# Attention with routed experts on one core: experts computed for the tokens that chose them, in 15 sorted tiles

## The chip, the core and the metric

The kernel runs on one core of one Trainium2 chip. Times are device microseconds of one execution. Three runs of the kernel before gave 1228.81, 1231.50 and 1231.53 us, so its median is 1231.5 us. The profile is of one further execution.

## The reference

The input is 8 batches of 512 tokens with 128 features. Each batch goes through differential causal attention with 16 heads of 8 features, then a layer norm, then a mixture of 8 experts of which each token takes the best two, then a last layer norm. Everything is float32.

```python
attn = softmax(s1) - lam * softmax(s2)              # causal, 16 heads
attn = attn / max(sum(abs(attn)), 1e-6)
x = layernorm(x + (attn @ v) @ Wo.T)
xn = layernorm(x) * gamma + beta
probs = softmax(xn @ router_w.T / 1.5)
w, idx = top_k(probs, 2)                            # 2 of E = 8 experts
h = silu(einsum('btd,edf->betf', xn, W1))           # 128 -> 512, every expert
y = einsum('betf,efd->betd', h, W2)                 # 512 -> 128
x = layernorm(x + x + sum over e of wdense[e] * y[e])
```

## The kernel before, in words

One batch of attention is cut into 64 units, one for a head and a tile of 128 queries. The program of each engine is a list of passages, and a passage has 64 slots; slot s issues the scores of unit s on TensorE, and behind it, at fixed lags, the maximum (VectorE, line 723), the exponentials (ScalarE, line 491), the scaling and subtraction of the two maps (GpSimd, lines 441 and 445, five slots later, so slot s treats unit s-5), the transposes and the product with the values. A unit's width runs over 256, 128, 384 and 512 keys, four units of each in turn.

The rest of the work is side tasks, which a table SIDE puts into slots. A passage b holds the attention of batch b, the preparation of batch b+1 ("prep", slots 24 to 43) and everything behind the attention of batch b-1 ("post", slots 8 on). Post tasks whose slot is 64 or more run in the next passage ("late"), so the experts of a batch lie across two passages. TensorE and ScalarE do a side task in its own slot, VectorE one slot later and GpSimd two slots later (LAG_SIDE). Each engine's queue is in order: an instruction that waits holds back all that stands behind it on that engine. The first attention passage (batch 0) has no post work; after the eighth, a passage with the end of the attention pipeline and one with late tasks alone follow.

The experts before take each of the 8 experts over all 512 tokens: 32 tasks "hidden" (a 512-column matmul on TensorE, line 803; tanh on ScalarE, line 537; the product hT on VectorE, line 686) and 32 tasks "expert" (4 matmuls of 128 columns each, line 809; acc on VectorE, line 698, with the gate, which is zero for tokens that did not choose the expert). They fill about one per slot from slot 20 to slot 84. A float32 matmul shows as two matmul records in the trace. The experts' matrices are loaded once, 4 MB, and stay in SBUF.

SyncE issues all transfers. It writes the split projections to DRAM (line 390, 13 transfers a batch) and reads them back as stacks (line 398, 36 transfers a batch); each group of nine stack transfers waits until the scores that read its buffer are done.

## Time and profile before

| | |
|---|---|
| median of 3 runs | 1231.5 us |
| the profiled execution | 1223.18 us, span of the trace 1221.3 us, granted clock 0.952 |
| first maximum of batch 0 | 38.5 us |
| passages of batches 0 to 7 | 103.5, 135.2, 140.4, 140.3, 140.2, 142.5, 140.4, 134 us |
| after the last maximum | 106.3 us |

The profiled execution is 1.9 us longer than its span. The passages are cut at VectorE's first maximum of a batch. Engines are PE (TensorE matmul), PEld (its weight load), DVE (VectorE), ACT (ScalarE), POOL (GpSimd) and SPq (SyncE's queue).

### The profile page before, as it was taken

How to read it: one execution, taken by the hardware profiler on the slowest of the kernel's cores; microseconds unless marked ns; L12 is line 12 of the kernel's file. 1: busy time of each engine (PE TensorE's matmuls, PEld its weight loads, DVE VectorE, ACT ScalarE, POOL GpSimd, SP SyncE). 2: the span in 40 equal slices, each digit the busy share in tenths (PEclk: the TensorE clock that was granted, in tenths of full speed). 3: DMA queues.
4: the chain of work that ended last, by engine and by line, in shares of the span. 5: the costliest groups of instructions: out<-in, count | busy, mean ns of one | idle time of the engine just before them, and what ended most of it. 6: DMA issues, size and time to landing. Idle time of an engine off the chain costs nothing.

```text
span 1221.3 us, 29361 instructions
## 1 busy us (share of the span) xinstructions
PE 1103.2 (90%) x8786; PEld 725.7 (59%) x8786; DVE 1044.4 (86%) x2722; ACT 915.2 (75%) x2882; POOL 834.0 (68%) x1245
## 2 busy tenths in 40 slices
PE   3788869999899989999899997999899998999897
PEld 1355536666556655666556665666556665566565
DVE  1688788988999899999999899999999999898664
ACT  1688868888688877888688876888678886787232
POOL 2599976776768757877667776777677777677100
PEclk8577779999999999999999999999999999999899
DMA  7503400232005200142003300052002410000000
GB/s 213 126 14 80 99 1 3 62 82 48 1 14 118 70 2 2 36 110 57 1 14 86 89 15 1 21 125 57 1 2 57 89 48 1 19 1 2 1 10 9
DMA packets 62142, 54.66 MB, mean 45 GB/s; under 512 B 6050, under 2 KB 59938, under 8 KB 61986
## 3 DMA queue, kind: packets, MB, share of 16 engines
q1 hardware_dynamic: 61986, 52.78, 17.8%
q8 instruction: 73, 1.20, 0.4%
q14 instruction: 83, 0.68, 0.2%
HBM read 37.03 MB, written 15.73 MB: 43 GB/s over the span
## 4 chain that ended last, share of the span: by engine, by line
PE 66%; DVE 18%; issue 7%; POOL 4%; ACT 2%; SPq 1%; DMA 1%; DVEq 0%; POOLq 0%; ACTq 0%
PE side L809 14%; PE side L803 13%; PE trans L883 12%; PE scores L853 8%; PE heads L872 7%; DVE neg_max L723 6%; PE scores L855 4%; DVE abs_sum L734 3%; PE scores L803 2%; PE scores L809 2%; POOL exps L445 2%; PE side L773 2%; DVE hT L686 1%; DVE xh L566 1%; POOL exps L441 1%
## 5 line engine op out<-in xcount | busy, mean ns | idle before, releaser
L491 ACT ACTIVATE exps<-scores,neg_max 128x256 f32<-128x256 f32 (+3 forms) x1024 | 537.9, 529 | 97.5 <-DVE neg_max L723 80.8
L723 DVE TENSOR_REDUCE neg_max<-scores 128x1 f32<-128x256 f32 (+3 forms) x1024 | 448.7, 479 | 72.8 <-PE scores L855 69.3
L445 POOL TENSOR_TENSOR exps<-exps 128x384 f32<-128x384 f32 (+3 forms) x512 | 444.7, 868 | 42.7
L441 POOL TENSOR_SCALAR exps<-exps,inv_l,lam_l 128x384 f32<-128x384 f32 (+3 forms) x512 | 313.6, 613 | 141.2 <-DVE inv_l L714 138.4
L853 PE MATMUL scores<-stack 72*128 72x256 bf16 (+3 forms) x1024 | 274.1, 314 | 17.5 <-DMA stack<-parts_dram 13.5
L809 PE MATMUL side<-w_sb,hT 128*128 128x128 f32 x1816 | 253.6, 283 | 29.5 <-DVE acc L698 18.1
L883 PE MATMUL trans<-ident,exps 128*128 128x128 f32 x1280 | 254.9, 300 | 22.8 <-ACT diffT L499 19.4
L499 ACT ACTIVATE diffT<-trans 128x384 f32<-128x384 f32 (+3 forms) x512 | 223.4, 436 | 52.9 <-PE trans L883 52.1
L809 PEld LDWEIGHTS side<-w_sb,hT 128*128 128x128 f32 x1816 | 222.6, 192 | 63.7 <-DVE acc L698 29.9
L803 PE MATMUL side<-xnT,w_sb 128*128 128x512 f32 x458 | 247.2, 621 | 1.8 <-ACT xnT L526 1.0
L883 PEld LDWEIGHTS trans<-ident,exps 128*128 128x128 f32 x1280 | 150.4, 147 | 134.7 <-issue 102.5
L855 PE MATMUL scores<-causal_bf,ident_bf 128*128 128x128 bf16 x1024 | 216.5, 228 | 0.0
L491 ACT ACTIVATION_READ_ACCUMULATOR exps<-scores,neg_max 128x1 f32 x1024 | 210.7, 206 | 0.0
L734 DVE TENSOR_REDUCE abs_sum<-exps 128x2 f32<-128x512 f32 (+3 forms) x256 | 206.9, 808 | 1.7 <-POOL exps L445 1.7
L686 DVE SCALAR_TENSOR_TENSOR hT<-tanh_sb,side 128x512 f32<-128x512 f32 x229 | 155.8, 680 | 36.3 <-ACT tanh_sb L537 34.5
L537 ACT ACTIVATE tanh_sb<-side 128x512 f32<-128x512 f32 x229 | 136.1, 594 | 48.0 <-PE side L803 44.8
L853 PEld LDWEIGHTS scores<-stack 72*128 72x128 bf16 x1024 | 108.2, 106 | 64.1 <-ACT exps L491 22.8
L872 PE MATMUL heads<-diffT,v_sb 128*32 128x128 f32 x2560 | 139.2, 291 | 0.0
L872 PEld LDWEIGHTS heads<-diffT,v_sb 128*32 128x32 f32 x2560 | 51.0, 109 | 122.2 <-ACT diffT L499 61.4
L855 PEld LDWEIGHTS scores<-causal_bf,ident_bf 128*128 128x128 bf16 x1024 | 105.4, 103 | 7.7
L437 POOL TENSOR_TENSOR lam_l<-sums,lam_all 128x4 f32<-128x4 f32 x128 | 25.9, 203 | 91.1 <-ACT exps L491 90.7
L803 PEld LDWEIGHTS side<-xnT,w_sb 128*128 128x128 f32 x458 | 69.3, 191 | 15.0 <-DVE hT L686 2.7
(94 smaller groups left out, 685.2 us busy)
## 6 DMA issues: line engine op xcount, KB each, us to landing
stack<-parts_dram SPq DMA_DIRECT2D x288, 96.0 KB
parts_dram<-parts SPq DMA_DIRECT2D x104, 128.0 KB, 2.4
x_in<-x_dram SPq DMA_DIRECT2D x8, 256.0 KB, 4.5
w_sb<-w_dram SPq DMA_DIRECT2D x1, 2048.0 KB, 9.1
x_res<-x_dram SPq DMA_DIRECT2D x8, 256.0 KB, 4.5
o_dram<-y_out SPq DMA_DIRECT2D x8, 256.0 KB, 3.4
wq_sb<-wqT_dram SPq DMA_DIRECT2D x1, 64.0 KB
wq_sb<-wk1T_dram SPq DMA_DIRECT2D x1, 64.0 KB
```

What stands on the lines that cost most here:

```text
L441: nc.gpsimd.tensor_scalar(diff[:, q % 2, j, 0:w], exps[:, q % 2, 1, j, 0:w], inv_l2[:, q % 2, j:j + 1], lam_l1[:, q % 2, j:j + 1], ALU.mul ...
L445: nc.gpsimd.tensor_tensor(diff[:, q % 2, j, 0:w], diff[:, q % 2, j, 0:w], exps[:, q % 2, 0, j, 0:w], ALU.subtract).then_inc(diff_done.sem, 1)
L491: nc.scalar.activation(exps[:, q % 2, k, j, 0:w], scores[:, u % 2, k, 0:w], ACT.Exp, bias=neg_max[:, q % 2, j, k:k + 1], accum_out=sums[:, ...
L499: nc.scalar.activation(diffT[:, q % 2, j, 0:w], trans[:, 0:w], ACT.Copy)\
L723: nc.vector.tensor_reduce(neg_max[:, q % 2, j, k:k + 1], scores[:, u % 2, k, 0:w], AX.X, ALU.max, negate=True).then_inc(max_done.sem, 1)
L734: nc.vector.tensor_reduce(abs_sum[:, q % 2, j - 1:j + 1], diff[:, q % 2, j - 1:j + 1, 0:w], AX.X, ALU.add, apply_absolute_value=True).then ...
L803: last = nc.tensor.matmul(bank[:, :], w1_sb[:, e, f * P:(f + 1) * P], xnT[:, :], start=True, stop=True)
L809: last = nc.tensor.matmul(bank[:, 0:D], hT[:, e % 2, f, t * P:(t + 1) * P], w2_sb[:, e, f, :], start=(f == 0), stop=(f == NF - 1))
L853: nc.tensor.matmul(scores[:, u % 2, k, 0:w], stack[:, 0, QUAD * g + j, t * P:(t + 1) * P], stack[:, 1 + k, QUAD * g + j, 0:w], start=True, ...
L855: nc.tensor.matmul(scores[:, u % 2, k, w - P:w], ident_bf[:, :], causal_bf[:, :], start=False, stop=True).then_inc(score_done.sem, 1)
L872: last = nc.tensor.matmul(heads[k * STRIP:(k + 1) * STRIP, t * P:(t + 1) * P], v_sb[:, i, NG * k + g, :], diffT[:, q % 2, k, i * P:(i + 1) ...
L883: last = nc.tensor.transpose(trans[:, i * P:(i + 1) * P], diff[:, q % 2, j, i * P:(i + 1) * P], ident[:, :])
```

## The change

The experts now work on sorted tokens. After routing, "count" and "place" compute with small matmuls and seven vector operations where each of the 1024 (token, expert) pairs of a batch goes, and which expert owns each of 15 tiles of 128 rows. GpSimd scatters the normalised tokens with 8 indirect transfers of 128 rows into a DRAM tensor; SyncE reads it back in 4 transfers ("sorted"); TensorE transposes it in 4 tasks "turn". Each tile then has one "hidden" (4 matmuls of 128 columns), one "expert" (4 matmuls) and, on SyncE, one "weights": a register is read from SBUF and 512 KB of the owner's matrices are fetched into one of 3 buffers. The outputs are written to DRAM in 4 transfers ("y_out"), gathered by 8 indirect transfers and added with the gates in 8 "combine". 32 tasks hidden and 32 expert a batch become 15 and 15. SyncE's list is now also written by slots.

```diff
-FIRST_EXPERT_SLOT = 20
-EXPERT_TASKS = (1, 2, 1, 1, 1, 1, 1, 1, 0, 1, 1, 1, 1, 1, 1, 1)
+COUNT_SLOT, PLACE_SLOT, SCATTER_SLOT, FIRST_TILE_SLOT = 27, 29, 31, 42
+WEIGHTS_AHEAD = 3
...
+    put(COUNT_SLOT, "post", "count")
+    put(PLACE_SLOT, "post", "place")
+    for i in range(TOP * NT):
+        put(SCATTER_SLOT + i, "post", "scatter", i)
+    put(SCATTER_SLOT + TOP * NT + 1, "post", "sorted")
+    for j in range(WEIGHTS_AHEAD):
+        put(FIRST_TILE_SLOT - 6 + j, "post", "weights", j)
+    for c, chunk in enumerate(CHUNKS):
+        put(FIRST_TILE_SLOT - 1 + 2 * chunk[0], "post", "turn", c)
+    slot = FIRST_TILE_SLOT
+    for j in range(TILES + 1):
+        if j < TILES:
+            put(slot + 2 * j, "post", "hidden", j)
+        if j:
+            put(slot + 2 * j + 1, "post", "expert", j - 1)
+            if j - 1 + WEIGHTS_AHEAD < TILES:
+                put(slot + 2 * j + 2, "post", "weights", j - 1 + WEIGHTS_AHEAD)
+    for c, chunk in enumerate(CHUNKS):
+        put(slot + 2 * chunk[-1] + 5, "post", "y_out", c)
+    slot += 2 * TILES + 4
+    for i in range(TOP * NT):
+        put(slot + i, "post", "gather", i)
+        put(slot + i + 2, "post", "combine", i)
+    slot += TOP * NT + 2
+    put(slot, "post", "norm3")
...
+                if name == "sorted":
+                    sp.wait_ge(scattered.sem, scattered.after(n, TOP * NT))
+                    sp.wait_ge(turned.sem, turned.after(n - 1, len(CHUNKS)))
+                    for c in CHUNKS:
+                        sp.dma_start(xg[:, c[0]:c[-1] + 1, :], pools(x_sorted[c[0] * P:(c[-1] + 1) * P, :]))\
+                          .then_inc(sorted_in.sem, 16)
+                if name == "weights":
+                    j = task[2]
+                    if j == 0:
+                        sp.wait_ge(placed.sem, placed.after(n, 6))
+                    m, k = (n, j - WEIGHTS_AHEAD) if j >= WEIGHTS_AHEAD else (n - 1, TILES + j - WEIGHTS_AHEAD)
+                    sp.wait_ge(y_copied.sem, y_copied.after(m, k + 1))
+                    which = sp.value_load(owner_int[0:1, j:j + 1], min_val=0, max_val=E - 1)
+                    sp.dma_start(w12_sb[:, j % WEIGHTS_AHEAD, :],
+                                 w12[bass.ds(which, 1), :, :].rearrange("o p f -> p (o f)"))\
+                      .then_inc(weights_loaded[j % WEIGHTS_AHEAD].sem, 16)
+                if name == "y_out":
+                    c = CHUNKS[task[2]]
+                    for i in range(TOP * NT) if n else ():
+                        sp.wait_ge(gathered[i].sem, gathered[i].after(n - 1, 1))
+                    sp.wait_ge(y_copied.sem, y_copied.after(n, c[-1] + 1))
+                    sp.dma_start(pools(y_dram[c[0] * P:(c[-1] + 1) * P, :]), y_sorted[:, c[0]:c[-1] + 1, :])\
+                      .then_inc(y_sorted_out.sem, 16)
...
+                    for task, n, _ in side_tasks(b, stages, slot):
+                        if task[0] == "post":
+                            sorted_part(task[1], n, task)
+                        if task[1] == "proj":
+                            parts_part(n, task[2])
+                    if "prep" in stages and slot >= PREP_SLOTS[3] + 5 and slot - PREP_SLOTS[3] - 5 < NG - 1:
+                        stack_part(b + 1, slot - PREP_SLOTS[3] - 5)
+                    if "prep" in stages and slot == UNITS - 1:
+                        stack_part(b + 1, NG - 1)
...
+            sp.wait_ge(consts_made, CONSTS)
+            sp.dma_start(pools(x_sorted), xg[:, :, :]).then_inc(sorted_cleared, 16)
...
+                        if name == "scatter":
+                            i = task[2]
+                            if i == 0:
+                                pool.wait_ge(sorted_cleared, 16)
+                                pool.wait_ge(sorted_in.sem, sorted_in.after(n - 1, len(CHUNKS)))
+                                pool.wait_ge(placed.sem, placed.after(n, 5))
+                                pool.wait_ge(xh_done.sem, xh_done.after(n, 1))
+                            nc.gpsimd.indirect_dma_start(
+                                x_sorted[:, :], bass.IndirectOffsetOnAxis(ap=place_int[:, i:i + 1], axis=0),
+                                xh[:, i % NT, :], None).then_inc(scattered.sem, 16)
+                        if name == "gather":
+                            i = task[2]
+                            if i == 0:
+                                pool.wait_ge(y_sorted_out.sem, y_sorted_out.after(n, len(CHUNKS)))
+                                pool.wait_ge(combined.sem, combined.after(n - 1, TOP * NT))
+                            nc.gpsimd.indirect_dma_start(
+                                y_back[:, i, :], None, y_dram[:, :],
+                                bass.IndirectOffsetOnAxis(ap=place_int[:, i:i + 1], axis=0)).then_inc(gathered[i].sem, 16)
...
                         if name == "expert":
-
-                            e, t = task[2], task[3]
+                            j = task[2]
                             dve.wait_ge(psum_of(task).sem, psum_of(task).after(n, psum_count[task]))
-                            if e == 0:
-                                dve.wait_ge(route_step.sem, route_step.after(n, ROUTE_STEPS))
-                                dve.wait_ge(acc_set.sem, acc_set.after(n, 1))
-                            else:
-                                dve.wait_ge(expert_done.sem, expert_done.after(n, NT * (e - 1) + t + 1))
+                            dve.wait_ge(y_sorted_out.sem, y_sorted_out.after(n - 1, len(CHUNKS)))
+                            nc.vector.tensor_copy(y_sorted[:, j, :], bank[:, 0:D]).then_inc(y_copied.sem, 1)
+                        if name == "combine":
+                            i = task[2]
+                            t = i % NT
+                            dve.wait_ge(gathered[i].sem, gathered[i].after(n, 1))
+                            dve.wait_ge(route_step.sem, route_step.after(n, ROUTE_STEPS))
+                            dve.wait_ge(acc_set.sem, acc_set.after(n, 1))
+                            if i >= NT:
+                                dve.wait_ge(combined.sem, combined.after(n, t + 1))
                             nc.vector.scalar_tensor_tensor(
-                                out=acc[:, t, :], in0=bank[:, 0:D], scalar=gates[:, t, e:e + 1],
-                                in1=(acc if e else x1_twice)[:, t, :], op0=ALU.mult, op1=ALU.add).then_inc(expert_done.sem, 1)
+                                out=acc[:, t, :], in0=y_back[:, i, :], scalar=gates[:, i // NT, t:t + 1],
+                                in1=acc[:, t, :] if i >= NT else x1_twice[:, n % 2, t, :],
+                                op0=ALU.mult, op1=ALU.add).then_inc(combined.sem, 1)
...
+                if name == "turn":
+                    c = CHUNKS[task[2]]
+                    pe.wait_ge(sorted_in.sem, sorted_in.after(n, len(CHUNKS)))
+                    for i, j in enumerate(c):
+                        last = nc.tensor.transpose(bank[:, i * P:(i + 1) * P], xg[:, j, :], ident[:, :])
                 if name == "hidden":
-                    e, f = task[2], task[3]
-                    if isinstance(n, int) and n == 0 and e == f == 0:
-                        pe.wait_ge(experts_in, 2 * 16)
-                    pe.wait_ge(xnT_copied.sem, xnT_copied.after(n, 1))
-                    last = nc.tensor.matmul(bank[:, :], w1_sb[:, e, f * P:(f + 1) * P], xnT[:, :],
-                                            start=True, stop=True)
+                    j = task[2]
+                    w = j % WEIGHTS_AHEAD
+                    pe.wait_ge(turned.sem, turned.after(n, j // NT + 1))
+                    pe.wait_ge(weights_loaded[w].sem, weights_loaded[w].after(n, j // WEIGHTS_AHEAD + 1))
+                    for f in range(NF):
+                        last = nc.tensor.matmul(bank[:, f * P:(f + 1) * P], w12_sb[:, w, f * P:(f + 1) * P], xgT[:, j, :],
+                                                start=True, stop=True)
                 if name == "expert":
-                    e, t = task[2], task[3]
-                    pe.wait_ge(hidden_done.sem, hidden_done.after(n, NF * (e + 1)))
+                    j = task[2]
+                    pe.wait_ge(hidden_done.sem, hidden_done.after(n, j + 1))
                     for f in range(NF):
-                        last = nc.tensor.matmul(bank[:, 0:D], hT[:, e % 2, f, t * P:(t + 1) * P],
-                                                w2_sb[:, e, f, :], start=(f == 0), stop=(f == NF - 1))
+                        last = nc.tensor.matmul(bank[:, 0:D], hT[:, (n * TILES + j) % 2, f, :],
+                                                w12_sb[:, j % WEIGHTS_AHEAD, F + f * D:F + (f + 1) * D],
+                                                start=(f == 0), stop=(f == NF - 1))
```

The order of the instructions changes at these places.

GpSimd at slots 33 to 35, before: `exps` are the probability maps, four units of 512 keys.

```order
L437 TENSOR_TENSOR lam_l<-sums,lam_all 128x4
L441 TENSOR_SCALAR exps<-exps,inv_l,lam_l 128x512
L445 TENSOR_TENSOR exps<-exps 128x512
L441 TENSOR_SCALAR exps<-exps,inv_l,lam_l 128x512
L445 TENSOR_TENSOR exps<-exps 128x512
```

The same place of GpSimd after, where `xh` are the normalised tokens and `place_int` the row numbers:

```order
L533 TENSOR_TENSOR lam_l<-sums,lam_all 128x4
L537 TENSOR_SCALAR exps<-exps,inv_l,lam_l 128x512
L541 TENSOR_TENSOR exps<-exps 128x512
L557 DMA x_sorted_dram<-xh,place_int 1920x128
L537 TENSOR_SCALAR exps<-exps,inv_l,lam_l 128x512
L541 TENSOR_TENSOR exps<-exps 128x512
L557 DMA x_sorted_dram<-xh,place_int 1920x128
```

An indirect transfer now stands behind each of eight units, the last at slot 40, and the next unit stands behind it; eight gathers stand so at slots 14 to 21.

TensorE at slots 41 and 42, after, where `xg` are the sorted tokens, and the scores below the transposes are those of slot 42:

```order
L1031 MATMUL scores<-stack 128x384
L1033 MATMUL scores<-causal_bf,ident_bf 128x128
L973 MATMUL side<-ident,xg 128x128 x4
L1050 MATMUL heads<-diffT,v_sb 32x128 x4
L1061 MATMUL trans<-ident,exps 128x128 x2
L1031 MATMUL scores<-stack 128x384
L1033 MATMUL scores<-causal_bf,ident_bf 128x128
L1031 MATMUL scores<-stack 128x384
L1033 MATMUL scores<-causal_bf,ident_bf 128x128
L980 MATMUL side<-xgT,w_sb 128x128 x4
```

The transposes of the sorted tokens stand ahead of the scores of slot 42; before, one 512-column matmul of the experts stood there, which waited for nothing new.

SyncE at slots 46 to 50, after, with what each instruction waits for; `w_sb` is the tile's matrices:

```order
L434 TENSOR_LOAD owner_int [waits y_copied]
L434 ISA x2
L435 ISA
L435 DMA w_sb<-w_dram 128x1024
L462 DMA stack<-parts_dram 24x4x512 [waits score_done,parts_out]
L462 DMA stack<-parts_dram 24x4x512 x8
L434 TENSOR_LOAD owner_int [waits y_copied]
L434 ISA x2
L435 ISA
L435 DMA w_sb<-w_dram 128x1024
```

Before, SyncE had no experts' transfer behind the first load; now each tile's fetch waits for the output copy three tiles back, and stack transfers stand between two fetches.

## Rows read from the trace of the kernel before

**Rows 1.** the page's part 1: busy us, share of the span, instructions
```profile
PE 1103.2 (90%) x8786; PEld 725.7 (59%) x8786; DVE 1044.4 (86%) x2722; ACT 915.2 (75%) x2882; POOL 834.0 (68%) x1245
```

**Rows 2.** the page's part 4: the chain that ended last, by engine
```profile
PE 66%; DVE 18%; issue 7%; POOL 4%; ACT 2%; SPq 1%; DMA 1%; DVEq 0%; POOLq 0%; ACTq 0%
```

**Rows 3.** windows of two passages: length, busy PE to POOL, clock, DMA, GB/s
```profile
38.50:142.00 103.50, 92.45 (x667) 52.39 (x665) 87.10 (x209) 90.03 (x317) 89.39 (x136) 0.71 0.32 70
...
557.90:698.10 140.20, 132.30 (x1098) 88.08 (x1098) 129.64 (x341) 113.89 (x361) 103.83 (x154) 1.00 0.19 46
```

**Rows 4.** the second passage in four windows, slots 10 on first; columns the same
```profile
578.40:623.90 45.50, 38.85 (x323) 25.10 (x321) 42.69 (x136) 31.33 (x99) 29.88 (x46) 1.00 0.01 2
...
623.90:651.80 27.90, 27.51 (x219) 18.23 (x217) 26.37 (x64) 24.07 (x77) 22.68 (x29) 1.00 0.10 26
...
651.80:698.10 46.30, 45.69 (x385) 30.09 (x383) 42.51 (x100) 41.38 (x130) 34.60 (x55) 1.00 0.37 89
...
557.90:578.40 20.50, 20.25 (x178) 14.66 (x179) 18.07 (x47) 17.11 (x57) 16.68 (x26) 1.00 0.29 77
```

**Rows 5.** groups by shape: busy, mean ns, idle before, releasers
```profile
L809 PE MATMUL side<-w_sb,hT 128*128 128x128 f32 x1816 | 253.6, 283 | 29.5 <-DVE acc L698 18.1 <-DVE hT L686 5.5 <-issue 5.3
...
L803 PE MATMUL side<-xnT,w_sb 128*128 128x512 f32 x458 | 247.2, 621 | 1.8 <-ACT xnT L526 1.0 <-DVE hT L686 0.5
...
L445 POOL TENSOR_TENSOR exps<-exps 128x512 f32<-128x512 f32 x128 | 163.3, 1276 | 10.7
...
L464 POOL TENSOR_TENSOR rstd<-var_eps,minus_half 128x4 f32<-128x4 f32 x24 | 24.5, 1019 | 1.9
```

**Rows 6.** the same windows, the gated sum's first half alone (hT, line 686)
```profile
578.40:623.90 45.50, 5.41 (x8) 1.00 0.01 2
...
623.90:651.80 27.90, 4.77 (x7) 1.00 0.10 26
```

**Rows 7.** the same windows, accumulation over experts alone (acc, line 698)
```profile
578.40:623.90 45.50, 3.06 (x9) 1.00 0.01 2
...
623.90:651.80 27.90, 2.35 (x7) 1.00 0.10 26
```

**Rows 8.** line 398, issue of one stack transfer by SyncE: ns min/median/max
```profile
L398 SPq DMA_DIRECT2D stack<-parts_dram x288: 290/375/1662, 30.9 to 981.6; - x144
```

**Rows 9.** GpSimd's timeline, slots 33 to 40: first and last piece
```profile
636.08 0.77 POOL L441 TENSOR_SCALAR exps<-exps,inv_l,lam_l 128x512 f32<-128x512 f32 x1 [0.84 <-DVE inv_l L714]
...
651.12 0.73 POOL L445 TENSOR_TENSOR exps<-exps 128x256 f32<-128x256 f32 x1
```

**Rows 10.** the page's part 6: issues, KB of one, median us to landing
```profile
parts_dram<-parts SPq DMA_DIRECT2D x104, 128.0 KB, 2.4
...
x_in<-x_dram SPq DMA_DIRECT2D x8, 256.0 KB, 4.5
...
w_sb<-w_dram SPq DMA_DIRECT2D x1, 2048.0 KB, 9.1
...
o_dram<-y_out SPq DMA_DIRECT2D x8, 256.0 KB, 3.4
```

**Rows 11.** the chain in order of time, first transfer: start, us
```profile
7.88 2.79 DMA x_in<-x_dram
```

**Rows 12.** the timeline at slot 42: start, length, engine, operation
```profile
652.90 0.33 PE L853 MATMUL scores<-stack 72*128 72x384 bf16 x1
```

**Rows 13.** the timeline in slots 50 and 52: VectorE's side task, TensorE's
```profile
670.65 0.35 DVE L698 SCALAR_TENSOR_TENSOR acc<-side,gates,acc 128x128 f32<-128x128 f32 x1
...
674.57 1.07 PE L803 MATMUL side<-xnT,w_sb 128*128 128x512 f32 x2
```

**Rows 14.** windows of the end, after the last maximum; columns the same
```profile
1115.00:1151.00 36.00, 31.40 (x258) 22.13 (x256) 25.36 (x68) 14.77 (x33) 16.34 (x20) 1.00 0.00 1
...
1151.00:1215.00 64.00, 61.02 (x328) 42.99 (x328) 36.01 (x96) 19.38 (x34) 1.20 (x2) 0.95 0.02 5
```

**Rows 15.** line 566, normalising, the form that writes xh: ns min/median/max
```profile
L566 DVE TENSOR_SCALAR xh<-x,mv,rstd x32: 333/344/1432, 179.9 to 1149.2; 128x128 f32<-128x128 f32 x32
```

More of the change, by code:

```diff
@@ L104 @@
 PREP_TASKS = [t for s in sorted(SIDE) for t in SIDE[s] if t[0] == "prep"]
-PSUM_TASKS = ("den_T", "out_proj", "xn_T", "logits", "hidden", "expert", "x_T", "proj", "values")
+PSUM_TASKS = ("den_T", "out_proj", "xn_T", "logits", "count", "place", "turn", "hidden", "expert",
+              "x_T", "proj", "values")
+EXPERT_PSUM = ("turn", "hidden", "expert")
 STORED = (0, 1, 2, 0, 1)
@@ L284, in reader @@
                 "proj": (rest_made, task[2] + 1) if name == "proj" else None,
[L285 to L286 removed]
+                "count": (counted, 1), "place": (placed, 2),
+                "turn": (turned, task[2] + 1) if name == "turn" else None,
+                "hidden": (hidden_done, task[2] + 1) if name == "hidden" else None,
+                "expert": (y_copied, task[2] + 1) if name == "expert" else None,
             }[name]
@@ L309, in build @@
             for experts in (False, True):
-                chosen = [t for t in tasks if t[1] in PSUM_TASKS and (t[1] in ("hidden", "expert")) == experts]
+                chosen = [t for t in tasks if t[1] in PSUM_TASKS and (t[1] in EXPERT_PSUM) == experts]
                 for n, t in enumerate(chosen):
@@ L314, in psum_of @@
         def psum_of(task):
-            if task[1] in ("hidden", "expert"):
+            if task[1] in EXPERT_PSUM:
                 return expert_psum
@@ new lines, in side_task @@
+                if name == "place":
+                    pe.wait_ge(counted.sem, counted.after(n, 1))
+                    nc.tensor.matmul(bank[:, 0:NT * E], before[:, :], hit[:, 2, :, :], start=True, stop=False)
+                    for s in range(1, NT):
+                        nc.tensor.matmul(bank[:, s * E:NT * E], ones[:, :], hit[:, 2, 0:NT - s, :], start=False, stop=False)
+                    for k in range(NT):
+                        nc.tensor.matmul(bank[:, 0:NT * E], full[:, k, :], start_sb[:, 0:NT, :],
+                                         start=False, stop=(k == NT - 1))
+                    for k in range(NT):
+                        last = nc.tensor.matmul(bank[:, NT * E:(NT + 1) * E], full[:, k, :], start_sb[:, NT, :],
+                                                start=(k == 0), stop=(k == NT - 1))
```

235 lines of the change are left out of this document (153 added, 82 removed).

## The prediction

> **What bounds the kernel now.** I read the page's busy shares first: TensorE 90%, VectorE 86% of the span [rows 1]. The chain that ended last agrees: two thirds of it is TensorE [rows 2]. Then I cut one passage (batch 4, 140.2 us) into four windows [rows 3, 4]: slots 10 to 27, 28 to 40, 41 to 63, and 0 to 9. The reader should see three different limits. In slots 41 to 63 TensorE is busy 45.7 of 46.3 us, in 0 to 9 20.3 of 20.5: every microsecond that TensorE waits there is lost. In 10 to 27, where norms and routing lie, VectorE is busy 42.7 of 45.5. In 28 to 40 TensorE again has 27.5 of 27.9. The passage without experts (batch 0) takes 103.5 us, with GpSimd busy 89.4 of them [rows 3]: take the experts away and GpSimd is nearly the next limit, though it looks idle for a third of the time on the page.
>
> **What is removed.** 17 of 32 "hidden" and 17 of 32 "expert" a batch. One hidden costs TensorE two records of 0.54 us, one expert eight of 0.14 (busy by count) [rows 5], so about 1.1 us each: 37 us a batch. But the remaining 30 tasks keep one per slot, in slots 42 to 73. A tile's hidden is eight records of 128 columns, the shape of the expert row, thus 1.1 us as well. So in slots 41 to 63 and 0 to 9 TensorE has as much to do as before, and the saving lies only in slots 10 to 40.
>
> **Slots 10 to 27.** Without experts VectorE has 42.7 - 5.4 - 3.1 = 34.2 us [rows 4, 6, 7], plus 8 combines at 0.34, what each of nine cost before, = 36.9. GpSimd has 29.9 plus 8 gathers. What GpSimd pays for one indirect transfer of 128 rows no row shows. Lower bound 0.4 us, what SyncE spends on a stack transfer [rows 8]; upper bound 2.6 us, twice GpSimd's longest operation of 1.28 (a list for the source and one for the destination). I take 1.2, near its costliest operation on a tiny tile (1.02 for 128x4) and on a wide one (1.28) [rows 5]. So 29.9 + 9.6 = 39.5 us, and at the 92% busy that such a limit reaches, 43 instead of 45.5: **-2.5 us** a batch. Combines wait for gathers one slot after their issue; GpSimd is ahead often enough that I add nothing.
>
> **Slots 28 to 40 and the turn.** GpSimd did slots 33 to 40 from 636.1 to 651.9, the first four wide ones [rows 9]. Eight scatters add 9.6; 1.7 of gaps in it and 1.5 of an earlier start (28 to 32 have no experts) come off: the last scatter ends at 658.2. Its landing takes 2.4, as SyncE's writes to DRAM do; then four reads of 256 KB: issue 0.45 each, landing 2.8 alone to 4.5 behind others, 5.0 together [rows 10, 11]. At 665.6 the transposes of slot 41 may start, 0.6 us, and only behind them the scores of slot 42, which started at 652.9 [rows 12]. 666.2 - 652.9 = **+13.3 us**. All of attention is behind it: maxima, exponentials and, in its next group of four units, GpSimd. The time does not come back, since TensorE fills the slots after it. Even with scatters at no cost, landing and read-back alone leave some 5 us. Three more turns cost four transposes each, half an expert's records, 0.55: **+1.7**. Clearing and count and place hide under GpSimd's scatters.
>
> **The fetches.** A tile's matrices are asked for when the output three tiles back is copied, on VectorE in slot s, and needed by TensorE in slot s+2. Today the same places are 671.0 (end of a side task, slot 50) and 674.6 (slot 52): 3.6 us of cover [rows 13]. The fetch takes 0.1 for the semaphore, 0.6 for the register (no row; 0 to 2.4, a round trip to DRAM), 0.5 to issue, and 3.7 to land, between 2.8 for 256 KB and 9.1 for 2048 KB [rows 10, 11]: 4.9. The missing 1.3 us is paid on every second tile, since a wait at one gives cover to the next: 0.65 on 12 tiles (3 are fetched early) = 8. Twice a batch nine or eighteen stack transfers at 0.38 [rows 8] stand before a fetch on SyncE, 3.4 or 6.8 us, of which I count 5 in all. **+13 us**; 0 if all lands in 3.6, 23 if a landing takes 4.5 and the register 1.0.
>
> **The clock.** TensorE is granted 1.00 (2.4 GHz) where it is busy, and 0.71, a mixture with 1.2 GHz, in the passage without experts [rows 3]. Waits of ten microseconds and lighter slots invite that. I charge 6% on the 67 us of slots 41 to 63 and 0 to 9: **+4 us**, bounds 0 and 16 (granted 0.8).
>
> **Start and end.** Before the first load SyncE now waits for GpSimd's constants and clears 1 MB: +3. The end has no attention to hide in. It took 36 + 64 us [rows 14] and the last norm. The first 36 hold the previous batch's gathers: +5. In place of the 64 (routing, count and place are my estimates for some thirty short operations in a row): routing 7, count and place 5, scatters 9.6 + 2.4, read-back 5, turn 1.5, first tile 4. Then the loop: from one output copy over the fetch (4.9), the next hidden (1.1), the expert behind it (1.1) to a copy (0.3) passes 7.4 us and two tiles, 3.7 each, times 14 = 52. Writing back 3.9 with its issue (3.4 at landing [rows 10]), gathers 9.6 + 2.4. Together 103: +39, so **+44** in all.
>
> **Sum.** A full passage: -2.5 + 13.3 + 1.7 + 13 + 4 = 29.5, six times (batches 2 to 7) = 177. Batch 1's passage has no slots 0 to 9 with experts: 24. With 3 and 44: 248. 1221.3 + 248 + 1.9 outside the span = 1471 on the profiled execution's scale of 1223.2; the median of the runs is 0.7% above that: **1480 us**.
>
> **A rule against the change.** The norm that writes xh usually takes 0.34 us and up to 1.43 [rows 15]: beside a GpSimd operation it is held until that one ends. If every scatter and gather is held or holds by such a 1.1, it is 16 x 1.1 x 7 = 123 us more, 1600 instead of 1480; it belongs to rival 2. The Trainium skill (SBUF — State Buffer, section "Who interferes with whom") says that VectorE's copies and scalar operations on SBUF and GpSimd's work lock each other out for a whole instruction, the writing of descriptors too. By that rule, the trace agrees on the lock, and no run here shows descriptors.
>
> **Rivals.**
> 1. The fetches are hidden, because they land in 3.6 us. For it: 2.8 for 256 KB alone [rows 11]. Against: the stack transfers between. Then 13 x 6.7 = 87 falls away, and at the end 14 x (3.7 - 2.4) = 18, where 2.4 is TensorE's own work on a tile: 1375. Chance 0.15.
> 2. An indirect transfer holds GpSimd 2.5 us, by itself or held by VectorE. Scatters +10.4; slots 10 to 27 then need 29.9 + 20 = 50 on GpSimd, 52 long, +9: 19.4 x 7 and 16 x 1.3 at the end, 157 more: 1640. Chance 0.17.
> 3. The clock is granted 0.8 in the slots that TensorE fills: +12 x 6.7: 1560. For it is the 0.71 [rows 3], against it that these slots keep TensorE busy. Chance 0.10.
> 4. Not slower: the waits are absorbed, and the busiest engine sets the pace as TensorE does now (132 of 140). GpSimd would have 103.8 + 19.2 = 123, at 93% a passage of 132, -8 x 7, with the end +44 and start: 1222. It needs the wait at slot 41 to be covered, which decides at about zero between scatter and transposes. Against it: seven microseconds of landings between two tasks that now lie within one. Chance 0.07.
> The forecast itself, 1400 to 1560: 0.51.
>
> **Range and chances.** Single bounds: an indirect transfer at 0.4 takes off 8 x 0.8 and 3.7 (VectorE then bounds slots 10 to 27 at 39.3) seven times and 13 at the end, 1397; fetches hidden give 1375, both near 1300; 2.6 gives 1650; the dearer fetch 1560. 1340 to 1650 holds the forecast, rivals 1, 3 and most of 2. Faster by over 0.3% (about what a measurement can tell from no change) only by rival 4, which is near no change: 0.05, same 0.02, slower 0.93.
>
> **What would show it.** TensorE idle some 13 us at slot 41, ended by the read-back. Waits at hidden for the matrices, every second tile. GpSimd's indirect transfers near 1.2 us. Passages near 170 us, of which slots 10 to 27 give 43. The end from 106 to 150 us. The prediction is wrong if the passages stay near 140, above all if TensorE finds the sorted tokens there.

## The result, and the profile after

The changed kernel takes **1641.2 us** (median of 4 runs, 1638.7 to 1652.6) against 1230.4 before (1228.8 to 1231.5): ratio 1.336, 95% interval 1.329 to 1.343. That is 411 us slower; 249 were forecast. The size lies inside the range by 9 us, but two terms of the sum were wrong in kind, not only in size.

The page's part 1 and three lines of part 2 (tenths in 40 slices) for the changed kernel answer [rows 1]:

```profile
PE 1111.0 (68%) x8522; PEld 794.6 (49%) x8522; DVE 953.7 (58%) x2585; ACT 866.2 (53%) x2778; POOL 977.2 (60%) x1385
...
PE   2988766776578584784947849578476875788262
...
PEclk8678657976579755996568965689567985589577
DMA  4323015510354003540126401353014520133243
```

264 matmul records have gone, yet TensorE's busy time rose by 8 us: the granted clock fell from 0.95 to 0.74 as a mean over the span. No engine is above 68%. The chain that ended last, 66% TensorE before [rows 2], now names everybody:

```profile
PE 30%; POOL 21%; DMA 16%; DVE 12%; SPq 9%; issue 9%; ACT 1%; DVEq 0%; POOLq 0%; ACTq 0%
```

Batch 4's passage in the same four windows as [rows 4] (slots 0 to 9, 10 to 27, 28 to 40, 41 to 63; length, busy PE to POOL, clock, DMA share, GB/s):

```profile
712.40:739.60 27.20, 22.33 (x200) 18.63 (x198) 16.20 (x43) 16.87 (x56) 16.43 (x25) 0.87 0.41 116
739.60:795.90 56.30, 31.99 (x245) 19.78 (x243) 40.10 (x129) 28.45 (x97) 39.23 (x55) 0.66 0.07 19
795.90:831.10 35.20, 29.66 (x171) 19.34 (x171) 20.87 (x56) 20.42 (x68) 25.66 (x31) 0.60 0.12 36
831.10:913.30 82.20, 55.21 (x455) 42.75 (x453) 41.38 (x96) 42.25 (x131) 40.59 (x61) 0.80 0.54 141
```

The passage takes 200.9 us instead of 140.2 [rows 3]. All four parts are longer: by 6.7, 10.8, 7.3 and 35.9. The windows of [rows 4] do not begin quite at the slots: in the trace before, the first maximum of slot 10 is at 577.9 and that of slot 28 at 624.7, not at 578.4 and 623.9. Between equal slots the four parts are longer by 7.2, 9.5, 8.0 and 35.9; as means over batches 2 to 6 by 7.4, 9.2, 8.0 and 33.0. Where nothing else is said, the numbers below go by [rows 4], as the forecast did.

No engine is busy for more than 85% of any part, where before the busiest had 94 to 99%. So most of the extra time is waiting; in slots 28 to 40 TensorE is also slower, busy for 29.7 us with 171 records where it was busy for 27.5 us with 219. The view of waits (engine, tile, who was waited for: us in total, times, longest) says for what:

```profile
PE side L973 <- DMA xg<-x_sorted_dram: 103.5, 7, 15.4
DVE acc L852 <- DMA y_back<-y_sorted_dram,place_int: 101.8, 43, 5.0
...
PE side L980 <- DMA w_sb<-w_dram: 96.4, 37, 6.7
PE side L947 <- DVE xh L689: 75.2, 8, 12.3
...
DVE place_of L809 <- PE side L967: 27.0, 7, 3.9
...
PE scores L973 <- DMA xg<-x_sorted_dram: 20.7, 1, 20.7
```

Three waits of about 100 us each: the turn for the sorted tokens, the combines for their gathers, the tiles for their matrices. A fourth, TensorE's wait at slot 19 for the normalised tokens xh, was 18.1 us in 8 waits before; it follows from the second, as shown below. The 20.7 us are the turn of the last batch.

**The turn.** TensorE's timeline around slot 41 (start, us, engine, operation), then GpSimd's and SyncE's:

```profile
846.58 1.09 PE L973 MATMUL side<-ident,xg 128*128 128x128 f32 x4 [15.18 <-DMA xg<-x_sorted_dram]
...
848.66 0.53 PE L1031 MATMUL scores<-stack 72*128 72x384 bf16 x1
```
```profile
836.36 1.08 POOL L557 DMA_INDIRECT x_sorted_dram<-xh,place_int  x1 [0.16 <-issue]
```
```profile
840.35 2.04 SPq L426 DMA_DIRECT2D xg<-x_sorted_dram  x4
```

The last scatter's instruction ends at 837.4, the read is issued from 840.4, and the transposes start at 846.6: 9.1 us between. Slot 41 took 18.3 us instead of 1.9. Place stands in the same line, at 797.3, with 24 records of TensorE at half clock:

```profile
797.30 0.58 PE L960 MATMUL side<-hit,before 128*128 128x32 f32 x2
797.69 1.43 PE L962 MATMUL side<-hit,ones 128*128 128x24 f32 x6
799.05 1.91 PE L964 MATMUL side<-start_sb,full 8*128 8x32 f32 x8
800.77 1.85 PE L967 MATMUL side<-start_sb,full 8*128 8x8 f32 x8
```

They take 5.3 us, some 0.22 a record, though the widest moves 32 columns. In these 5.3 us the loading of TensorE's weights is busy for 5.25.

**The combines** on VectorE, slots 16 to 19:

```profile
765.29 0.62 DVE L852 SCALAR_TENSOR_TENSOR acc<-y_back,gates,x_twice 128x128 f32<-128x128 f32 x1 [4.52 <-DMA y_back<-y_sorted_dram,place_int]
...
769.95 0.75 DVE L852 SCALAR_TENSOR_TENSOR acc<-y_back,gates,acc 128x128 f32<-128x128 f32 x1 [2.52 <-DMA y_back<-y_sorted_dram,place_int]
```

and GpSimd at the same place:

```profile
760.31 0.78 POOL L537 TENSOR_SCALAR exps<-exps,inv_l,lam_l 128x512 f32<-128x512 f32 x1 [2.74 <-DVE inv_l L869]
761.17 1.27 POOL L541 TENSOR_TENSOR exps<-exps 128x512 f32<-128x512 f32 x1
762.59 1.04 POOL L565 DMA_INDIRECT y_back<-y_sorted_dram,place_int  x1 [0.15 <-issue]
```

Behind the waiting combines stand the maxima of the slots and the norm that writes xh, so ScalarE, GpSimd and TensorE wait as well. TensorE's part of it:

```profile
773.09 1.09 PE L947 MATMUL side<-ident,xh 128*128 128x128 f32 x4 [9.95 <-DVE xh L689]
```

A gather costs GpSimd as much as a scatter (ns min/median/max):

```profile
L557 POOL DMA_INDIRECT x_sorted_dram<-xh,place_int x64: 964/1082/1240, 221.2 to 1552.6; - x64
L565 POOL DMA_INDIRECT y_back<-y_sorted_dram,place_int x64: 945/1046/1257, 353.8 to 1627.8; - x64
```

**The fetches.** SyncE's queue in slots 50 to 54 and what TensorE waited for there:

```profile
868.04 6.61 SPq L462 DMA_DIRECT2D stack<-parts_dram  x15
875.69 3.52 SPq L435 DMA_DIRECT2D w_sb<-w_dram  x2
```
```profile
885.41 2.05 PE L980 MATMUL side<-xgT,w_sb 128*128 128x128 f32 x8 [6.48 <-DMA w_sb<-w_dram]
```
```profile
L434 SPq TENSOR_LOAD <-owner_int x120: 262/270/838, 216.8 to 1607.3; - x120
```
```profile
DMA to landing us min/median/max: 3.1/3.8/6.9
```

The last fence is the time from issue to landing, for the 40 of the 120 matrix loads whose landing the view gives; by the last landing mark of each, all 120 take 3.1 to 9.6 us, 3.7 in the middle. One fetch alone costs what was forecast: 0.3 for the register, 0.3 for the issue, 3.8 to land. The long wait comes where the stack transfers stand ahead of it, and there the fetch is late twice: the output it waits for was copied at 869.3, the fetch was issued at 875.7, behind them on SyncE, and it took 9.6 us to land, at 885.3, the longest of all.

### The profile page after: what moved, and what is told of

Read it like the earlier page. It is cut to its first block, busy times and chain, and to the rows that moved or that the text cites. A ratio compares the mean times of both kernels' runs of the same rounds, so it can differ in the third digit from the quotient of the medians.

```text
span 1637.5 us, 29253 instructions
## 1 busy us (share of the span) xinstructions
PE 1111.0 (68%) x8522; PEld 794.6 (49%) x8522; DVE 953.7 (58%) x2585; ACT 866.2 (53%) x2778; POOL 977.2 (60%) x1385
## 3 DMA queue, kind: packets, MB, share of 16 engines
q1 hardware_dynamic: 110866, 128.23, 27.8%
## 4 chain that ended last, share of the span: by engine, by line
PE 30%; POOL 21%; DMA 16%; DVE 12%; SPq 9%; issue 9%; ACT 1%; DVEq 0%; POOLq 0%; ACTq 0%
POOL exps L541 8%; DMA w_sb<-w_dram 8%; POOL exps L537 6%; PE side L980 5%; SPq L462 5%; PE trans L1061 5%; DVE neg_max L878 4%; PE scores L1031 4%; POOL x_sorted_dram L557 4%; PE heads L1050 3%; PE side L986 3%; DMA y_back<-y_sorted_dram,place_int 3%; DMA xg<-x_sorted_dram 2%; DMA x_sorted_dram<-xh,place_int 2%; PE scores L1033 2%
## 5 line engine op out<-in xcount | busy, mean ns | idle before, releaser
L1061 PE MATMUL trans<-ident,exps 128*128 128x128 f32 x1280 | 308.2, 351 | 141.5 <-ACT diffT L613 95.2
L1031 PE MATMUL scores<-stack 72*128 72x256 bf16 (+3 forms) x1024 | 327.2, 364 | 19.1 <-DMA stack<-parts_dram 15.8
L1033 PE MATMUL scores<-causal_bf,ident_bf 128*128 128x128 bf16 x1024 | 248.6, 257 | 0.0
L980 PE MATMUL side<-xgT,w_sb 128*128 128x128 f32 x864 | 140.8, 314 | 97.1 <-DMA w_sb<-w_dram 96.4
L980 PEld LDWEIGHTS side<-xgT,w_sb 128*128 128x128 f32 x864 | 123.0, 219 | 111.2 <-issue 106.4
L1031 PEld LDWEIGHTS scores<-stack 72*128 72x128 bf16 x1024 | 125.0, 122 | 78.8 <-ACT exps L605 32.8
L836 DVE SCALAR_TENSOR_TENSOR hT<-tanh_sb,side 128x512 f32<-128x512 f32 x108 | 74.2, 687 | 133.2 <-ACT tanh_sb L658 130.6
L658 ACT ACTIVATE tanh_sb<-side 128x512 f32<-128x512 f32 x108 | 64.5, 597 | 160.8 <-PE side L980 159.5
L986 PE MATMUL side<-w_sb,hT 128*128 128x128 f32 x864 | 131.1, 299 | 5.1 <-DVE hT L836 5.1
L1033 PEld LDWEIGHTS scores<-causal_bf,ident_bf 128*128 128x128 bf16 x1024 | 122.1, 119 | 15.7
L986 PEld LDWEIGHTS side<-w_sb,hT 128*128 128x128 f32 x864 | 116.1, 209 | 13.6 <-DVE hT L836 8.4
L565 POOL DMA_INDIRECT y_back<-y_sorted_dram,place_int x64 | 68.1, 1065 | 86.9 <-DMA y_sorted_dram<-y_sorted 75.5
```

What stands on the lines that cost most here:

```text
L980: last = nc.tensor.matmul(bank[:, f * P:(f + 1) * P], w12_sb[:, w, f * P:(f + 1) * P], xgT[:, j, :], start=True, stop=True)
L986: last = nc.tensor.matmul(bank[:, 0:D], hT[:, (n * TILES + j) % 2, f, :], w12_sb[:, j % WEIGHTS_AHEAD, F + f * D:F + (f + 1) * D], start=( ...
L1031: nc.tensor.matmul(scores[:, u % 2, k, 0:w], stack[:, 0, QUAD * g + j, t * P:(t + 1) * P], stack[:, 1 + k, QUAD * g + j, 0:w], start=True, ...
L1033: nc.tensor.matmul(scores[:, u % 2, k, w - P:w], ident_bf[:, :], causal_bf[:, :], start=False, stop=True).then_inc(score_done.sem, 1)
L1061: last = nc.tensor.transpose(trans[:, i * P:(i + 1) * P], diff[:, q % 2, j, i * P:(i + 1) * P], ident[:, :])
```

## The experiments

Each was timed beside the kernel before on the same chip, in three rounds (the last four in five); that kernel gave 1230.1, 1233.1 and 1234.5 us on the three chips used. Ratios to it have 95% intervals in brackets. "Less" is against 1641.2 us, or the run named, and across chips it is good to some 5 us.

**1. The combines three slots later** (and all that follows them):

```
- put(slot + i + 2, "post", "combine", i)      + put(slot + i + 5, "post", "combine", i)
- slot += TOP * NT + 2                         + slot += TOP * NT + 5
```

> Each combine stands three slots later behind its gather; nothing else moves. If the waits in line theory holds, VectorE's 102 us of waiting for gathers (43 waits, longest 5.0 us) were all on the path in slots 12 to 20: those slots fall from 33 us to about 24, and the time from 1641 to about 1570. If GpSimd's own work sets the pace there (16 indirect transfers of 1.07 us), the waits only move to another engine and the time changes by less than 15 us.

Measured: 1590.6 us, 1.292 [1.288, 1.296]: 51 less, 20 short of the 71 expected. The wait fell from 101.8 to 12.4:

```profile
DVE acc L852 <- DMA y_back<-y_sorted_dram,place_int: 12.4, 9, 4.9
```

Slots 16 to 19 went from 18.0 to 12.3 us, and TensorE's wait for xh from 75.2 to 40.0. The wait was real, but 89 us less of it were worth 51 us of time; some reappeared in other waits, the matrices' among them (96 to 103).

**2. The turn eight slots later**, and with it all that follows (tiles, gathers, combines), with gates and places in two buffers so that the next batch can write its own:

```
- FIRST_TILE_SLOT = 27, 29, 31, 42             + FIRST_TILE_SLOT = 27, 29, 31, 50
- gates = sb("gates", [P, TOP, NT])            + gates = sb("gates", [P, 2, TOP, NT])
- place_int = sb("place_int", [P, TOP * NT])   + place_int = sb("place_int", [P, 2, TOP * NT])
...
```

> The tiles and the first turn start 8 slots later (50 instead of 42), the scatters stay; gates and row numbers get two buffers. Waits in line theory: TensorE's wait for the sorted tokens, 15 us a passage (124 us in all), goes away in the passages and stays only in the end: about 1641 - 7 x 15 = 1535. Rival (the backlog of GpSimd holds attention anyway once eight scatters are in its queue): half of it comes back as waits for GpSimd, about 1590. Second rival (stack transfers still fall between the fetches, only earlier in the row of tiles): no effect on the turn wait, but fetch waits change by up to 5 us a passage.

Measured: 1503.5 us, 1.223 [1.220, 1.227]: 138 less, the most of any single edit that leaves the sorting in, and 32 more than expected. The turn waits only in the last batch:

```profile
PE side L973 <- DMA xg<-x_sorted_dram: 22.6, 1, 22.6
```

The edit also moves the combines from slots 15 to 22 to slots 23 to 30, so the norm that writes xh no longer stands behind them: TensorE's wait for xh fell from 75.2 to 27.8 (two lines, the second for the last batch) and the waits for gathers from 101.8 to 61.4. That is the likely reason for the surplus; this run alone doesn't part the two effects. Slots 28 to 40 took 36.4 us, where they had taken 35.2: what scatters and place cost there isn't a matter of the turn.

**3. Five matrices ahead instead of three**, the room for them found by letting y_sorted share xg's memory (SyncE then also waits for the previous write back before it reads the tokens):

```
- WEIGHTS_AHEAD = 3                            + WEIGHTS_AHEAD = 5
- y_sorted = sb("y_sorted", [P, TILES, D])     + y_sorted = xg
```

> Five buffers for the tiles' matrices instead of three, so a fetch is asked for five tiles ahead; sorted inputs and outputs share one tensor to make room. If the missing cover of the fetches costs what TensorE's waits show (96 + 13 us), the time falls to about 1535, and slots 48 to 55, 31 us now, to about 17. Rival: the low clock and not the fetches makes these slots long: the waits go away and TensorE's instructions fill the time, about 1600.

Measured: 1531.0 us, 1.244 [1.241, 1.248]: 110 less, as expected, 23 of them behind the last maximum (149.5 to 126.5). Waits for matrices fell to a fifth (96.4 to 20.4), slots 48 to 55 of batch 4 from 31.5 us to 15.7, and its slots 42 to 63 from 63.9 us to 53.6; before the change they took 44.4.

**4. The stack transfers apart**, one group of nine in slots 47, 53 and 59 instead of 47, 48 and 49.

> SyncE issues the three stack groups of nine transfers at slots 47, 53 and 59 instead of 47, 48 and 49, so one group at most stands before a fetch. If the long wait in slots 50 to 55 (22 us against 8 before the change) is 18 stack transfers standing before a fetch, it shrinks to that of one group: 6 to 8 us a passage less, about 1590. If the fetch waits come from the short cover of two slots alone, the same 96 us of waits stay, spread over more tiles, within 10 us of 1641.

Measured: 1624.5 us, 1.315 [1.310, 1.320]: 17 less, between the two numbers expected and a miss for both. The longest wait fell from 6.7 to 4.1, the sum only from 96.4 to 79.5:

```profile
PE side L980 <- DMA w_sb<-w_dram: 79.5, 41, 4.1
```

The stack transfers are what makes a few waits long; most of the sum is the ordinary fetch, which with three buffers starts too late.

**5. Plain transfers in place of the indirect ones**, issued by SyncE to fixed rows. The tokens are then not sorted, and the result is not the reference's; the rest of the work is the same.

> The 8 scatters and 8 gathers a batch are plain transfers of the same size that SyncE issues to fixed rows; GpSimd issues none. So the tokens are not sorted, and each tile's rows are not those of its expert. Waits in line theory: the last row block lands about 10 us earlier, gathers land sooner: 8 to 14 us a passage less, about 1560, and TensorE still waits 5 us or more at the turn. GpSimd theory (16 x 1.3 us a passage set the pace): 20 us a passage less or more, 1480 or below.

Measured: 1496.6 us, 1.216 [1.211, 1.220]: 145 less, between the two theories. GpSimd's 137 us are gone, but so are nearly all waits for gathers (101.8 to 4.9), so on this kernel the edit mixes two causes. Experiment 10 parts them.

**6. TensorE kept busy before the turn**, by seven matmuls of 512 columns whose result is overwritten:

```
+ if task[2] == 0:
+     for _ in range(7):
+         nc.tensor.matmul(bank[:, :], wq_sb[:, 0, :], xT[:, :], start=True, stop=True)
```

> TensorE multiplies seven times over 512 columns (results are overwritten by the transposes) while it would wait for the sorted tokens; 7.5 us of work at 2.4 GHz, 15 at 1.2. If the low clock behind the idle wait costs time, slots 42 to 50 run at a granted clock near 1.0 instead of 0.8 and each passage is 2 to 4 us shorter: about 1620. If the clock costs nothing because TensorE waits anyway, no change; and if the idle wait is not what lowers the clock, the granted clock stays at 0.74 and the time may rise by a few us a passage.

Measured: 1644.0 us, 1.332 [1.327, 1.337]: no change. The mean clock rose only to 0.757, and the trace says where. TensorE's timeline in batch 4, then windows of slot 41 and of slots 42 to 44:

```profile
835.72 8.50 PE L973 MATMUL side<-xT,wq_sb 128*128 128x512 f32 x14
850.80 1.11 PE L976 MATMUL side<-ident,xg 128*128 128x128 f32 x4 [6.58 <-DMA xg<-x_sorted_dram]
```
```profile
835.60:853.65 18.05, 11.47 (x33) 5.28 (x32) 1.02 (x2) 2.15 (x7) 9.65 (x16) 0.69 0.53 160
853.65:863.08 9.43, 9.43 (x68) 6.76 (x66) 7.06 (x16) 6.29 (x20) 1.36 (x2) 0.80 0.10 27
```

The seven matmuls ran right behind slot 41's first work and were done 6.6 us before the tokens came, so the clock rose in slot 41, where there was nothing to gain, and was down again when slot 42 began: slots 42 to 44 were granted 0.80, as without the edit, and took 9.4 us, as without it. So the edit did not do what it was for, and its result does not price a low clock behind the wait. One batch hints at the answer: in batch 3 slots 42 to 44 got 0.95 for 0.82 and took 8.1 us for 9.3, and slots 45 to 49 took 11.7 for 10.3.

**7. What can the saved matmuls be worth?** The kernel before with four of its eight experts, one task in every second slot; the other four are left out.

```
- for e in range(E + 1):                       + for e in range(EX + 1):          # EX = 4
- EXPERT_TASKS = (1, 2, 1, 1, 1, 1, 1, 1, 0, 1, 1, 1, 1, 1, 1, 1)
+ EXPERT_TASKS = (1, 0)
...
```

> The kernel before with 4 of its 8 experts (the other 4 are left out of the sum), one task in every second slot: 32 tasks a batch instead of 64, and no sorting. It shows what the saved matmuls alone are worth. By the windows of the profile before, VectorE without half of its expert work needs about 113 us and GpSimd 104 a passage, TensorE 97: passages near 122 us instead of 140, the end 32 us shorter, about 1070. Rival: the norms and routing bound slots 10 to 27 so that little is gained there: passages of 130, about 1125.

Measured: 1137.2 us, 0.922 [0.919, 0.925], near the rival; five of its full passages take 132 to 134 us. Halving the expert work with no sorting, no fetches and no round trips gives 96 us: 7 to 10 in each full passage, 39 in the last batch with its end (201.2 for 240.3). Slots 10 to 27 gain nothing by it (47.6 us for 47.3, means of batches 2 to 6), though there are 4 products hT in them instead of 9, and 286 matmul records instead of 334 (batch 4). VectorE is then the busiest engine:

```profile
PE 912.1 (81%) x7506; PEld 580.0 (51%) x7506; DVE 938.7 (83%) x2466; ACT 839.8 (74%) x2754; POOL 834.5 (74%) x1245
```

So what the change takes out is worth about 8% in this arrangement of the tasks, and its own costs had to stay under that. Another arrangement might give more; none was tried.

**8. Four edits together**: 1, 2, 3 and 4.

> The turn late, five buffers, the stack groups apart and the combines late, all together. If the waits in line add up as they were measured one by one (138 + 110 + 50 and a few for the stacks), the time is about 1340, passages 150 us, still above the kernel before, because the end and GpSimd's transfers stay. Rival: with those waits gone another one takes their place (TensorE for GpSimd's transfers, or the low clock) and only two thirds of the sum arrive: about 1440.

Measured: 1345.5 us, 1.088 [1.085, 1.093]: 296 less. The four alone add up to 316, so they are nearly independent. What they leave in this kernel's waits:

```profile
PE side L974 <- DMA xg<-x_sorted_dram: 22.0, 1, 22.0
...
PE side L981 <- DMA w_sb<-w_dram: 17.2, 16, 2.4
DVE acc L853 <- DMA y_back<-y_sorted_dram,place_int: 11.3, 8, 5.0
```

**9. A short place**, in the changed kernel and in the combined one:

```
+ nc.vector.tensor_reduce(full_sum, full.rearrange("e k p -> e p k"), AX.X, ALU.add)
- for k in range(NT): nc.tensor.matmul(bank[:, 0:NT * E], full[:, k, :], ...)
- for k in range(NT): nc.tensor.matmul(bank[:, NT * E:(NT + 1) * E], full[:, k, :], ...)
+ nc.tensor.matmul(bank[:, 0:NT * E], full_sum[:, :], ...)
+ nc.tensor.matmul(bank[:, NT * E:(NT + 1) * E], full_sum[:, :], ...)
...
```

> The changed kernel, but VectorE adds up the four full-tile marks of an expert first (one reduction of 8 rows, waited for), so that the place task needs 6 fp32 matmuls instead of 12: the 6 that go were 12 of 24 records, 0.36 to 0.40 us each by their two groups, which overlap; some 2.8 us of TensorE's line a batch. Theory (place stands in line on TensorE ahead of the scatters, and so ahead of the turn): 1641 - 8 x 2.8 + 8 x 0.4 for the reduction = about 1620. Rival (place is hidden under other work, as the forecast had it): 1641, no change.

> The combined kernel (turn late, five matrices ahead, stack apart, combine late) with the short place: by the same theory 1345.5 - 19 = about 1326; if place is hidden once the turn no longer waits for the scatters, 1345.

Measured: 1620.3 us, 1.313 [1.311, 1.316], 21 less as the theory had it: place stands in line. In the combined kernel 1341.1 us, 1.087 [1.084, 1.089], against 1.088 [1.085, 1.093]: no difference that can be told, the rival's answer.

**10. Plain transfers in the combined kernel**, without and with the short place.

> The combined kernel with the 16 indirect transfers of a batch issued by SyncE as plain ones to fixed rows (tokens then aren't sorted; the rest of the work is the same). The turn and the combines no longer wait for them, so what is left is GpSimd's own 16 x 1.08 = 17 us a batch, of which the passage waits at GpSimd in some slots only. Theory (GpSimd's time is a part of what remains): about 5 us a passage, 1305. Rival (the transfers cost by the waits for their data alone, which are gone in the combined kernel): 1345, no change.

> The combined kernel with both, the short place and the plain transfers (tokens not sorted): if both theories hold and the two add, 1345.5 - 19 - 40 = about 1286, still above the kernel before; if neither does, 1345.

Measured: 1287.0 us, 1.042 [1.040, 1.045], 58 less than the combined kernel of experiment 8: the theory's direction, 18 more than its size. Here the waits for gathers are 5.0 against 11.3, so most of it is not the wait for their data but GpSimd's own time: at most 7 us a batch for 17 us of instructions. At most, because the matrices' waits (17.2 to 4.8) and the last turn's (22.0 to 15.9) fell too. With both edits 1274.8 us, 1.032 [1.028, 1.036], 11 less than if both theories held. Its page shows GpSimd back at its old load:

```profile
PE 1029.1 (81%) x8426; PEld 729.5 (58%) x8426; DVE 978.5 (77%) x2593; ACT 861.3 (68%) x2778; POOL 837.5 (66%) x1257
```

Even so it is 3% slower than the kernel before. Two of its windows, slots 10 to 27 and 28 to 40, against [rows 4]:

```profile
595.50:643.20 47.70, 36.52 (x306) 25.62 (x304) 39.77 (x120) 30.13 (x100) 28.64 (x44) 0.79 0.08 22
643.20:675.90 32.70, 24.77 (x164) 15.68 (x162) 27.52 (x73) 19.81 (x66) 23.24 (x30) 0.68 0.14 40
```

These are the slots from which expert work was taken, and they are 2.2 and 4.8 us longer than before with no engine full and the clock at 0.79 and 0.68; between equal slots 0.9 and 5.5. Whether the clock or the chain through routing and place holds them wasn't separated. In experiment 7, which has neither place nor scatters, slots 28 to 40 took 25.4 us at a clock of 0.95, here 32.8 at 0.64 (means of batches 2 to 6).

## Why the prediction was right, and where it was not

Right: direction, start, end and the price of single pieces. The end was forecast at 150 us and takes 149.5. An indirect transfer was taken at 1.2 us of GpSimd and costs 1.05 to 1.08. A fetch was put at 4.9 us and is about 4.7. Start: +1.7 for +3.

Measured over the whole span: start +2, batch 0 -3, batch 1 +41 (forecast 24), batches 2 to 6 +288 (148), batch 7 +42 (29.5), end +46 (44). For the last two the trace before is divided at its true last maximum, 1117.8: its last passage is 136.8 us and its end 103.5, not 134 and 106.3 as in the table above. So the end met its number from a lower start, and grew by 2 us more than forecast.

Step by step, batch 4's passage (forecast +29.5, measured +60.7):

- **Slots 10 to 27, forecast -2.5, measured +10.8: the failed step.** "Combines wait for gathers one slot after their issue; GpSimd is ahead often enough that I add nothing." It isn't ahead. The combine above had waited since 760.8; its gather started on GpSimd at 762.6, behind two pieces of attention of which the first had itself waited, and landed 2.7 us later (2.5 to 2.7 for the 32 gathers whose landing the view gives). Meanwhile the combine stands in VectorE's queue ahead of the maxima and of the norm for slot 19's transposes, for which TensorE waited 9.95 us. Experiment 1 takes the wait away and gets 51 us back. The gain of 2.5 was wrong too: it took VectorE's busy share for the limit of these slots. With the waits covered (experiment 8) they take 46.5 us for 47.3 before, with half the expert work simply left out (experiment 7) 47.6.
- **Slots 28 to 40 and the turn, forecast +13.3, measured +7.3 and +16.4.** The mechanism was right: scatter, landing, read-back, transposes, in this order, in front of slot 42's scores. Experiment 2 moves the consumer, and the wait is gone. Wrong was "Clearing and count and place hide under GpSimd's scatters": they come before the scatters and stand in the queues of TensorE and VectorE ahead of attention. The scatters did not wait for them directly: the row numbers were ready at 803.7, and the first scatter started at 814.0, with no wait, behind its unit of attention, which was late. Halving place's matmuls gives 21 us back, and gives nothing once the turn is late (experiment 9). From the start of slot 28 the scores of slot 42 came 10.5 us later than forecast: 5.2 of it before GpSimd reached the unit ahead of the first scatter, 2.1 in the stretch of the scatters, 1.7 in the landings (9.1 us, forecast 7.4), 1.5 between the transposes and the scores, at the lower clock level.
- **Fetches, turns and clock, forecast 18.7, measured 26.2** (slots 42 to 63 +19.5, 0 to 9 +6.7). Batch 4 is the longest passage; as a mean of batches 2 to 6 these slots grew by 23.9. The mechanism and the price were right: the fetches were put at 13 x 6.7 and 18 at the end, 105 us, and five buffers give 110 back. The split was not: spreading the stack transfers gives only 17 us, where 5 a batch were counted for them, so the ordinary fetch was too cheap. With five buffers slots 42 to 63 still take 52.6 us for 44.5 before (means), with a wait of 4.6 for one fetch among them; what the rest of that is was not traced.
- **The clock, forecast 0.94 in the tile slots, measured 0.80 in slots 41 to 63 and 0.66 and 0.60 in the lighter ones.** The windows of slots 41 to 63 show what it did (41; 42 to 44 and the start of 45; on into slot 51; to the end of 53; the rest):

```profile
831.10:849.40 18.30, 3.12 (x19) 1.75 (x18) 1.00 (x2) 2.12 (x7) 9.60 (x16) 0.50 0.52 158
849.40:860.20 10.80, 10.79 (x75) 7.48 (x74) 8.42 (x18) 7.65 (x23) 2.38 (x4) 0.82 0.19 51
860.20:878.90 18.70, 13.76 (x117) 11.48 (x116) 10.97 (x26) 11.23 (x37) 13.85 (x16) 0.91 0.86 179
878.90:891.80 12.90, 6.42 (x42) 5.85 (x42) 3.14 (x9) 3.19 (x12) 2.76 (x6) 0.74 0.58 141
891.80:913.30 21.50, 21.13 (x208) 16.19 (x207) 17.85 (x42) 18.06 (x57) 12.01 (x21) 1.00 0.45 139
```

0.50, the lower level of 1.2 GHz, while TensorE waits; a mixture in the busy stretch behind it; 1.00 once it has stayed busy. What the clock costs stays open, behind the turn as in the light slots: experiment 6 did not raise it where it could have counted.

The rivals: number 1 (fetches hidden) is false. Number 2 gave 1640, the measured time, by a mechanism that isn't there: no indirect transfer took over 1.26 us. A hold between VectorE and the transfers exists, and is far too small; it stands under the hardware below. The upper end of the range, 1650, was that same price, a transfer of 2.6 us, so it is luck that 1641 lies inside. Number 3 (clock at 0.8) had the level nearly right and its price is untested. Number 4 needed the turn covered; experiments 2 and 8 covered it and were still slower: experiment 7 puts the gain at 96 us, and the indirect transfers alone take back up to 58.

Where the 411 us are: the edits of experiment 8 recover 296, indirect transfers in that kernel 58, place some 12 more (1287.0 to 1274.8, intervals that don't touch). 40 stay, beside the 96 that experiment 7 offered and this kernel never got.

## What to carry to other kernels

When work goes through memory and back inside a pipeline that issues in order, first ask how many slots lie between the producer's last instruction and its first reader, and move the reader by the length of the whole chain (here 9.1 us for scatter and read-back, 2.6 from the start of a gather, which can itself be late: combines waited up to 5.0): this costs buffers, not time. A fetch whose address is only known at run time needs depth before anything else; spacing its queue is worth a sixth of that. Before building the sorted version at all, time the old kernel with the saved work simply left out: here that gave 8%, 96 us, and with the round trips mostly covered the sixteen indirect transfers a batch still cost up to 58.

## What the runs showed of the hardware

- An indirect transfer of 128 rows holds GpSimd 1.05 to 1.08 us, 0.94 at least and 1.26 at most. It costs at most about 0.4 of that in the time of a kernel whose GpSimd is busy 72% (experiment 8 against 10).
- An indirect transfer and a norm on VectorE can hold each other, for a part of the transfer. In each of six passages a norm that writes xh started 0.26 us into a gather and took 333 to 334 ns; the next started 0.51 us into it, took 917 or 918 ns and ended 0.17 to 0.18 us behind the gather; and these six gathers took 1254 to 1257 ns, where most transfers take 1040 to 1100. In the kernel of experiment 8 six combines that started 0.27 us into a gather took 683 to 689 ns, twice the usual. In the changed kernel the 7 combines that start within a transfer take 342 to 353 ns, and 48 maxima no more than 676, against 693 elsewhere. The Trainium skill (SBUF — State Buffer, section "Who interferes with whom") counts the writing of descriptors among what VectorE's copies lock out; these rows agree that the two exclude each other, but not for the whole of a transfer. In the changed kernel it is 0.6 us of VectorE six times in the run, where the forecast's dearer case had 1.1 us sixteen times a batch.
- Small fp32 matmuls are not small in time: records of 8 to 32 columns take some 0.22 us each at the lower clock level, 24 of them 5.3 us, and the weight loads are busy for 5.25 of these.
- TensorE's busy time is no measure of its work: with 3% fewer records it rose by 8 us, as the granted clock went from 0.95 to 0.74. The scores' matmuls took 364 ns a record on average (L1031), 314 before (L853).
- With five buffers a matrix took longer to land (4.7 us in the middle of 120 against 3.7, the longest 9.5 and 9.6) and the kernel was 110 us faster: landing time that nobody waits for costs nothing.
